# A decoder layer with attention and 16 experts: row numbers and gates copied out of the x buffers, a table in pieces, w2 loaded in seven parts

## What is computed

```python
x = x + attention_1(layernorm(x))                     # a linear attention
x = x + cross_attention(layernorm(x), ctx, ctx)       # 16 heads of 64, causal softmax
h = layernorm(x)
logits = h @ router_w + router_b                      # 16 experts
topw, topi = top_k(softmax(logits), 4); topw = topw / sum(topw)
for e in range(16):                                   # w1: 256x512, w2: 512x256
    out += (gelu(h @ w1[e] + b1[e]) @ w2[e] + b2[e]) * combine[:, e]
x = x + out
```

## Time and profile before

| | us |
|---|---|
| median of 3 runs (lowest, highest) | 1790.92 (1786.67, 1793.47) |
| the profiled execution | 1796.25 |
| its span in the trace | 1794.5 |
| busy in the span: PE, DVE, ACT, POOL | 1619.9, 1185.7, 1073.4, 504.7 |

### The profile page before, as it was taken

How to read it: one execution, slowest core, us unless ns; L and a number is a source line. 1 busy time by engine, 2 the same in 40 slices (tenths; PEclk the granted TensorE clock), 3 DMA queues, 4 the chain that set the end, 5 groups by cost and what they waited for, 6 DMA issues and landing times. The chain is left out here.

```text
span 1794.5 us, 35579 instructions
## 1 busy us (share of the span) xinstructions
PE 1619.9 (90%) x12470; PEld 1353.1 (75%) x12470; DVE 1185.7 (66%) x2675; ACT 1073.4 (60%) x2699; POOL 504.7 (28%) x430
## 2 busy tenths in 40 slices
PE   5899889999999999999999999657989989889995
PEld 4888767777776777777767777447989989888885
DVE  6988766677677776776677766557555555555552
ACT  4555466766666666766676666444556656555563
POOL 2444300001302103012021030315444444444544
PEclk9999999999999999999999999858999999999998
DMA  3121110000201101001011010726787776676773
GB/s 93 36 83 71 61 35 1 1 25 4 83 1 44 44 1 63 24 17 71 1 50 37 1 63 1 235 78 162 179 204 157 163 157 147 152 160 144 153 160 60
DMA packets 94926, 144.52 MB, mean 81 GB/s; under 512 B 12528, under 2 KB 55072, under 8 KB 94752
## 3 DMA queue, kind: packets, MB, share of 16 engines
q1 hardware_dynamic: 64128, 101.40, 18.8%
q0 software_dynamic: 28896, 38.62, 11.6%
q10 hardware_dynamic: 1728, 2.23, 0.4%
HBM read 90.76 MB, written 51.46 MB: 79 GB/s over the span
## 5 line engine op out<-in xcount | busy, mean ns | idle before, releaser
L1299 ACT ACTIVATE xa_prob<-xa_S,xa_nmax 128x512 f32<-128x512 f32 (+3 forms) x512 | 265.9, 534 | 135.0 <-DVE xa_nmax L1409 123.7
L1695 PE MATMUL ex_H<-ex_xT,ex_w 128*128 128x256 f32 x1896 | 254.4, 292 | 5.7 <-DVE ex_xT L1774 5.7
L1695 PEld LDWEIGHTS ex_H<-ex_xT,ex_w 128*128 128x128 f32 x1896 | 240.1, 198 | 6.5 <-issue 6.5
L1709 PE MATMUL ex_Y<-experts_w_hi,ex_hT 128*128 x1264 | 239.6, 283 | 0.0
L1780 DVE TENSOR_TENSOR ex_hT<-ex_h,ex_hT 128x512 fp32r<-128x512 f32 x158 | 109.4, 693 | 154.9 <-ACT ex_hT L1735 142.5
L1409 DVE TENSOR_REDUCE xa_nmax<-xa_S 128x2 f32<-128x1024 f32 (+3 forms) x256 | 197.7, 813 | 8.6 <-remote 5.0
L1709 PEld LDWEIGHTS ex_Y<-experts_w_hi,ex_hT 128*128 128x128 f32 x1264 | 200.4, 189 | 0.0
L1569 POOL DMA_INDIRECT expert_rows<-kept_xn,kept_rows x116 | 112.1, 967 | 292.4 <-DVE xa_prob L1421 252.2
L1313 ACT ACTIVATE xa_probT<-xa_work 128x512 f32<-128x512 f32 x256 | 139.9, 602 | 82.5 <-PE xa_work L1184 80.1
L1709 PE MATMUL ex_Y<-experts_w_lo,ex_hT 128*128 x632 | 178.6, 283 | 0.0
L1421 DVE TENSOR_SCALAR xa_prob<-xa_prob,xa_sums 128x512 f32<-128x512 f32 (+3 forms) x512 | 169.4, 384 | 6.8
(11 more groups left out here) (352 smaller groups left out, 3764.7 us busy)
## 6 DMA issues: line engine op xcount, KB each, us to landing
ahead_ctx<-in_w SPq DMA_DIRECT2D x27, 512.0 KB, 3.9
ahead_x<-in_w SPq DMA_DIRECT2D x26, 512.0 KB, 4.1
ahead_xn<-in_w SPq DMA_DIRECT2D x26, 512.0 KB
kept_x<-expert_rows SPq DMA_DIRECT2D x32, 273.0 KB, 3.1
kept_xn<-expert_rows SPq DMA_DIRECT2D x31, 273.0 KB
experts_w_lo<-in_w SPq DMA_DIRECT2D x4, 2048.0 KB, 9.5
ex_x<-expert_rows SPq DMA_DIRECT2D x16, 273.0 KB
expert_rows<-ahead_spare SPq DMA_DIRECT2D x32, 136.5 KB
```

The lines of the kernel that those rows point to most:

```text
L1299: m = act.activation(prob[n % 2][:, odd, PROB_AT[i]:PROB_AT[i] + width], SB[slot[at]][:, odd, col:col + width], ACT.Exp, bias=nmax[n % 2][ ...
L1695: m = pe.matmul(bank[:, (f % 2) * ROWS:(f % 2 + 1) * ROWS], ww[:, c, f * P:(f + 1) * P], xx[:, c, :], start=(i == 0), stop=(i == len(terms ...
L1709: m = pe.matmul(bank[:, a * D:(a + 1) * D], hh[:, f, a * P:(a + 1) * P], W2[:, bass.ds(own * WE + f * D, D)], start=(i == 0), stop=(i == l ...
```

## The change

It does the following.

1. Copies. In the step `transpose` of tile j, DVE first copies the row numbers and gates (17 columns of each of the two rows per partition) from the x buffer into one of five `tail`s, after waiting for x of tile j and for the add of tile j-5. ACT and GpSimd read gates and row numbers from there. The load of x into the buffer of tile j-5 waits for PE's transposes and for this copy, and no longer for the eviction of y and the add.
2. The late table. `work_out` is cut into `count_tiles`, `find_owners` and `find_rows`, done by DVE after steps 5, 7 and 9; PE's transposes follow in step 12, ahead of tile 12's hidden matmuls, DVE's copies at the end of step 12, and PE's transposes of tile 14 wait for them. Padding moves one step back.
3. The first table. It is worked out after the turns of pair 63, and turned and copied behind the last norm (`tables_turn`), with `first_loads` behind it.
4. w2. Seven loads of two or three experts, in the last batch's pairs 4 to 7, each after the projections and scores that use its place. The casts go in the order 3, 4, 5, 6, 7, 14, 15, 0, ...: four ahead of pair 63's weighing, eight behind it, four behind the last x transposes. 13 of 16 low halves are formed ahead of the barrier, three behind it, after step 0's low halves.
5. The barrier. SP waits for b1T, which it loads ahead of the barrier, and not for the store of x2; ACT waits for that store before its first eviction of y. The gelu table is loaded ahead of the barrier. Tiles and buffers change places in SBUF so that the store and the load of b1T run into nothing in use.

The diff, cut to its core:

```diff
+        self.used, self.warm = sb("used", [P, E]), sb("warm", [P, 1])
+        self.b1T = ahead.bits[:].rearrange("p a b -> p (a b)").bitcast(F32)[:, 0:E * FC]
...
-    def work_out(self, dve, w, done, part, ahead, kept, count):
+    def count_tiles(self, dve, w, done, part, kept, count):
...
+    def find_owners(self, dve, w, done, part, number, kept):
...
+    def find_rows(self, dve, w, done, part, number, kept, count):
...
-W2_LOADS, LOW_W2 = 4, 10
+LOAD_W2 = ((2, 5), (5, 8), (12, 14), (14, 16), (8, 10), (10, 12), (0, 2))
+OF_LOAD = {e_: i for i, (first, last) in enumerate(LOAD_W2) for e_ in range(first, last)}
+W2_ORDER, LOW_W2 = (3, 4, 5, 6, 7, 14, 15, 0, 1, 2, 8, 9, 10, 11, 12, 13), 13
...
-            plan += turns + finish + scatters
+            plan += [*turns, ("tables", None), *high_w2(0, 4), finish[0], *low_w2(0, 3), finish[1], *scatters]
...
-        elif p == 6:
-            second.append(("load_w2", None))
-        elif p == 7:
-            second.append(("tables", None))
+        else:
+            second += {4: [("load_w2", 0)], 5: [("load_w2", 1)], 6: [("load_w2", i) for i in (2, 3)],
+                       7: [("load_w2", i) for i in (4, 5, 6)]}.get(p, [])
...
-             *(("high_w2", e_) for e_ in range(E)), *low_w2(0, 3), ("output", (b, 1, 0)), *low_w2(3, 5), ("output", (b, 1, 1)),
-             ("first_loads", None), ("find3", b), ("norm3", b), ("transpose_x3", (b, 0)), ("transpose_x3", (b, 1)),
-             *low_w2(5, LOW_W2), ("route", b), ("choose", b), ("mark", b), ("weigh_gates", b), ("place", b), ("turn_gates", b),
+             *high_w2(4, 12), *low_w2(3, 6), ("output", (b, 1, 0)), *low_w2(6, 8), ("output", (b, 1, 1)), ("find3", b), ("norm3", b),
+             ("tables_turn", None), ("first_loads", None), ("transpose_x3", (b, 0)), ("transpose_x3", (b, 1)),
+             *high_w2(12, E), *low_w2(8, LOW_W2), ("route", b), ("choose", b), ("mark", b), ("weigh_gates", b), ("place", b), ("turn_gates", b),
...
-                    w.wait_ge(q_pe, B * PAIRS - 1)
...
+                    end, (first, last) = B * PAIRS - 1, LOAD_W2[at]
+                    w.wait_ge(k_pe, end - PAIRS)
+                    w.wait_ge(v_pe, v_tiles[-1])
+                    w.wait_ge(k_pe, end, at >= 2)
+                    w.wait_ge(s_pe, (end - 1, 1, 1), at >= 3)
+                    w.wait_ge(q_pe, end, at >= 4)
+                    w.wait_ge(s_pe, (end, (3, 2, 1)[at - 4], 1) if at >= 4 else None, at >= 4)
+                    sp.dma_start(f32(W2_lo[:, first * WE:last * WE]).rearrange("p (k n) -> p k n", n=D),
+                                 d['w2'][first:last].rearrange("e (k p) n -> p (e k) n", p=P)).then_inc(w2_in[at].of(at), 16)
                 elif step == "first_loads":
+                    w.wait_ge(pos_pe, B - 2)
+                    sp.dma_start(kept.b1T, d['b1T']).then_inc(b1_in.of(0), 16)
...
-            w.wait_ge(x2_out, B - 1)
+            w.wait_ge(b1_in, 0)
...
-                    w.wait_ge(pv_pe, (B * PAIRS - 1, 1))
-                    w.wait_ge(w2_in[at * W2_LOADS // E], at * W2_LOADS // E)
+                    w.wait_ge(s_pe, (B * PAIRS - 1, 1, 1))
+                    w.wait_ge(pv_pe, (B * PAIRS - 2, 1))
+                    w.wait_ge(pv_pe, (B * PAIRS - 1, 1), W2_ORDER.index(at) >= 4)
+                    w.wait_ge(w2_in[OF_LOAD[at]], OF_LOAD[at])
...
+                    if b == B - 1:
+                        act.activation(kept.warm[:], number[:], ACT.Gelu)
...
-                    tables.work_out(dve, w, t_dve, 0, ahead, kept, routing["count"])
+                    tables.count_tiles(dve, w, t_dve, 0, kept, count)
+                    tables.find_owners(dve, w, t_dve, 0, number, kept)
+                    tables.find_rows(dve, w, t_dve, 0, number, kept, count)
+                elif step == "tables_turn":
...
-        plan = [("load_w1", 2), ("load_x", 2), ("split_w1", 0), ("transpose", 0), ("split_w1", 1), ("load_w1", 3), ("low_w2", None)]
+        plan = [("load_x", 2), ("load_w1", 2), ("split_w1", 0), ("transpose", 0), ("split_w1", 1), ("load_w1", 3), ("load_x", 3)]
+        late = {5: ("count_tiles", None), 7: ("find_owners", None), 9: ("find_rows", None)}
         for j in range(MOE_TILES + 1):
-            plan += [("load_x", 3)] if j == 0 else []
-            plan += [(step, at) for step, at in (("load_w1", j + 4), ("load_x", j + 4), ("transpose", j + 1), ("hidden", j),
-                                                 ("split_w1", j + 2), ("results", j - 1)) if 0 <= at < MOE_TILES]
-            plan += [("tables", None)] if j == 4 else []
-            plan += [("pad", e_) for e_ in (2 * (j - 5), 2 * (j - 5) + 1) if 0 <= e_ < E]
+            step_of = {"load_w1": j + 4, "load_x": j + 4, "transpose": j + 1, "hidden": j, "split_w1": j + 2, "results": j - 1}
+            for step, at in step_of.items():
+                plan += [(step, at)] if 0 <= at < MOE_TILES else []
+                plan += [("turn_tables", None)] if step == "transpose" and j == TURN_AT else []
+                plan += [("low_w2", e_) for e_ in W2_ORDER[LOW_W2:]] if step == "hidden" and j == 0 else []
+            plan += [("give_tables", None)] if j == TURN_AT else []
+            plan += [late[j]] if j in late else []
+            plan += [("pad", e_) for e_ in (2 * (j - 6), 2 * (j - 6) + 1) if 0 <= e_ < E]
...
-            sp.dma_start(b1T, d['b1T']).then_inc(b1_in.of(0), 16)
...
-                    w.wait_ge(y_ev, j - NX, j >= NX)
-                    w.wait_ge(added[(j - NX) % NY], (j - NX, RT - 1), j >= NX)
+                    w.wait_ge(tail_set, j - NX, j >= NX)
...
-                if step == "tables":
-                    w.wait_ge(x_hi, 4)
-                    w.wait_ge(x_lo, 4)
+                if step == "turn_tables":
+                    w.wait_ge(x_hi, TURN_AT)
+                    w.wait_ge(x_lo, TURN_AT)
                     tables.transpose(pe, w, t_dve, XB[0], ident).then_inc(tables_pe.of(0), 1)
                 elif step == "transpose":
                     bank = XB[j % 2]
                     w.wait_ge(x_loaded[j % NX], j, j >= FIRST)
                     w.wait_ge(x_lo, j - 2, j >= 2)
-                    w.wait_ge(t_dve, ("landed", 2), j == 6)
+                    w.wait_ge(t_dve, ("landed", 2), j == TURN_AT + 2)
...
+                    w.wait_ge(x2_out, B - 1)
                     w.wait_ge(added[j % NY], (j - NY, RT - 1), j >= NY)
-                    w.wait_ge(x_loaded[j % NX], j, j >= FIRST)
+                    w.wait_ge(tail_set, j)
                     w.wait_ge(t_dve, ("landed", 2), j >= SURE_TILES)
                     own = act.value_load(owner_i[0:1, j:j + 1], min_val=0, max_val=E - 1)
                     for a in range(RT):
                         i = act.activation(y[j % NY][:, a, :], YB[j % 2][:, a * D:(a + 1) * D], ACT.Copy,
-                                           scale=x_in[j % NX][:, a, bass.ds(own + GATE, 1)])
+                                           scale=tail[j % NT][:, a, bass.ds(own + GATE - D, 1)])
...
-                    for e_ in range(LOW_W2, E):
...
-                elif step == "tables":
+                    mine = slice(j * WE, (j + 1) * WE)
+                    dve.tensor_tensor(W2_lo[:, mine], f32(W2_lo[:, mine]), f32(W2_hi[:, mine]), op=ALU.subtract
+                                      ).then_inc(low_w2.of(j), 1)
+                elif step == "count_tiles":
                     dve.tensor_tensor(pad_i[:], routing["count"][0:1, :], ahead.region[:], op=ALU.add).then_inc(pad_at.of(0), 1)
-                    tables.work_out(dve, w, t_dve, 1, ahead, kept, routing["count"])
+                    tables.count_tiles(dve, w, t_dve, 1, kept, routing["count"])
+                elif step == "find_owners":
+                    tables.find_owners(dve, w, t_dve, 1, ahead.number, kept)
+                elif step == "find_rows":
+                    tables.find_rows(dve, w, t_dve, 1, ahead.number, kept, routing["count"])
+                elif step == "give_tables":
                     w.wait_ge(tables_pe, 0)
                     tables.give_out(dve, t_dve, 1, XB[0], ahead, routing)
                 elif step == "split_w1":
                     w.wait_ge(w1_loaded[j % NW], j, j >= FIRST)
-                    w.wait_ge(b1_in, 0)
...
+                    w.wait_ge(x_loaded[j % NX], j, j >= FIRST)
+                    w.wait_ge(added[(j - NT) % NY], (j - NT, RT - 1), j >= NT)
+                    dve.tensor_copy(tail[j % NT], x_in[j % NX][:, :, D:PAY]).then_inc(tail_set.of(j), 1)
...
-                    w.wait_ge(x_loaded[j % NX], j, j >= FIRST)
+                    w.wait_ge(tail_set, j)
...
-                        pool.indirect_dma_start(out, bass.IndirectOffsetOnAxis(x_in[j % NX][:, a, ID:ID + 1].bitcast(I32), 0),
+                        pool.indirect_dma_start(out, bass.IndirectOffsetOnAxis(tail[j % NT][:, a, 0:1].bitcast(I32), 0),
```

(12 more changed lines are left out.)

64 lines of the change are left out of this document (27 added, 37 removed).

## The result

The changed kernel takes **1733.04 us** (median of 4 runs, 1730.92 to 1737.16), where the kernel before takes 1788.80 beside it: a ratio of 0.969, 95% interval 0.966 to 0.972. The forecast was 1728, from 1714 to 1753. In three later groups of runs on other chips the same pair gave 0.965 (0.960 to 0.970), 0.967 (0.964 to 0.970) and 0.972 (0.969 to 0.976). So the sign, the size and the range held, and each time the gain is between 50 and 60 us where 62.7 was forecast.

A forecast was written before the change was run, and what follows sets the result against it. In the expert stage the loop of x loads waiting for scatter-adds, not PE, was taken to set the pace (6.95 us a tile against 6.18). The terms summed to -62.7 from 1790.92, giving 1728 us, range 1714 to 1753.

The forecast's parts named there:

- The x loads, -54.6: Expert tiles: x loads wait for DVE's tail copy instead of an add, so all 45 PE waits, 54.6 us, go.
- What comes late next, +8 (5 to 14): Tiles 41 to 60: chained adds fall 18 us behind PE; part is borne, 8 us of stalls stay.
- the slack: Tail copy on DVE: 4 us spare before the add is awaited, about 4 more before PE needs DVE; 8 to 13 borne.
- The late table, -9.3 + 3 + 1.5: Tiles 6 and 7 gain 9.3 us; the turn at tile 12 costs 3, pieces sticking out of DVE's free time 1.5.
- the step of 9 us at tile 13: Expert tiles: sign of a right forecast, one step of about 9 us at tile 13.
- Pads, +3: Expert tiles that store pads: denser DMA keeps eight steps from quite running at PE's pace, +3 us (0 to 6).
- Handover, -12 (7 to 16): From attention to experts: later first table -8, turns and clock -5.5, w2 casts ahead of an eviction +1.5; 12 us gained.
- The 4.5 us for the five turns and 1 for the clock: Handover: 4.5 us back from ACT's five slow evictions if PE keeps its clock, 1 from the output projection.
- the handover gives nothing: Rival: slow turns have an unnamed cause, half clock may stay, casts may cost what the table did; 1740 us, chance 0.07.
- Barrier, 0: Barrier before the experts: SP's removed wait was hidden by GpSimd's drain, so nothing gained, at most 0.3 us.
- Opening, -2.3 (0 to 4): First expert tiles: b1T already there and fewer low halves give 5 us, later x for tile 4 takes 2.5 back.
- The rival of adds that become the bound: Rival, 16 chained expert-stage adds: each takes 1 us longer to land, 16 us more, 1744 us; chance 0.21.

The follow-up runs named there:

- second profile of before: The unchanged kernel before, run and profiled again on a quicker chip: 1787.17 us, ratio to itself 1.0006; handover 61.8 us.
- 4th of the changed kernel: The changed kernel unaltered, profiled a fourth time, as reference on a chip where the kernel before takes 1805.2 us: 1754.89 us, ratio 0.972.
- (d): Group of runs on one chip: the kernel before, nothing changed, once more for a second profile: 1787.17 us, ratio to itself 1.0006.
- (a): Group of runs on one slower chip: the changed kernel, unaltered, as reference 1746.34 us, the kernel before 1805.6 us.
- (b): Group of runs on one quicker chip: the changed kernel, unaltered, as reference 1732.55 us, the kernel before 1789.0 us.
- (c): Group of runs on one slower chip: the changed kernel, unaltered, as reference 1754.89 us, the kernel before 1805.2 us.

## Why the prediction was right, and where not

**The x loads, -54.6: the right cause.** All waits went. Putting the wait for the add back costs 36 (profiles) to 48 us (medians); by the sum it would be 43.6, the 54.6 less the 8 for late adds and the 3 for pads. The size of the one term is not shown: it is the idle time of the weight loads, and that of the matmuls behind them was 45.3.

**What comes late next, +8 (5 to 14): the right thing, forecast at less than half its size.** The main place, the engine and the order of events were as forecast: the adds of tiles 41 to 60 fall behind, DVE stops at the tail's copy, PE behind it. But it costs 17 to 23 us at tiles 54 to 67, and 3 to 7 at tile 12, which the sum did not have. Two steps of the sum failed. The first is the slack: 8 to 13 us were to be borne. PE first stops at tile 54 or 55, when the adds are some 9 us behind, so that much is right; but with the stop the chain itself becomes slower. From the first add of tile 40 to that of tile 60 it takes 140.0 us in the kernel with the copy two tiles later and 141.0 and 141.2 with four y buffers, close to the forecast 142; in the changed kernel it takes 145.3 to 150.7. The likely reason is in these rows of DVE and GpSimd:

```profile
1570.94 0.18 DVE L1804 COPY ahead_bits<-kept_xn 128x34 f32<-128x34 f32 x1 [5.70 <-DMA out<-ex_y,ahead_bits]
1571.04 0.68 DVE L1806 TENSOR_TENSOR ex_xT<-ex_X,ex_xT 128x512 fp32r<-128x512 f32 x1
...
1571.64 1.28 DVE L1812 TENSOR_TENSOR ex_hT<-ex_h,ex_hT 128x512 fp32r<-128x512 f32 x2
1571.73 2.10 POOL L1844 DMA_INDIRECT out<-ex_y,ahead_bits  x1 [5.13 <-POOLq L1840]
...
1572.84 0.90 DVE L1793 CAST ex_w<-ahead_ctx 128x1024 fp32r<-128x1024 f32 x1
1573.78 1.23 DVE L1795 TENSOR_TENSOR ex_w<-ahead_ctx,ex_w 128x1024 fp32r<-128x1024 f32 x1
1574.14 2.30 POOL L1844 DMA_INDIRECT out<-ex_y,ahead_bits  x1 [0.30 <-issue]
...
1574.92 0.16 DVE L1800 COPY ex_b<-ahead_bits 128x4 f32 x1
```

When the adds are that late, DVE and GpSimd wait for the same landing. Both start within 0.8 us of each other, DVE with everything that has piled up, and the two issues take 2.10 and 2.30 instead of 1.55. Over the adds of tiles 41 to 61 a mean issue is 1.86 to 1.90 us in the changed kernel, 1.68 in before, and 1.75 where the copy stands two tiles later; for the 40 issues of 20 tiles the last difference makes 4 to 6 us (an estimate), of the 5 to 11 by which the chain is longer. Such issues are no novelty: 2.30 stands at 1576.51 in before too. New is that DVE's wait makes them come one after the other. The Trainium skill, "SBUF — State Buffer", section "Who interferes with whom", has the rule by which copies on DVE hold up GpSimd's descriptors. The first issue agrees with it: a cast overlaps it and itself takes 0.90 instead of 0.69. The second does so less plainly, since beside it stand only the end of a subtraction and a copy of 0.16; which of DVE's instructions holds an issue up, no run separates. The prediction applied the rule to the new copy of the tail alone, and not to the burst that the new wait lets loose.

The second failure is the opening. The adds of tiles 1 to 7 are late as well: their first issues come 27 to 33 us after their tile's transposes, where 21 is undisturbed; in the code each of tiles 1 to 4 waits for the adds before it, up to two, whatever its expert. The longest wait of DVE at the copy up to tile 12 is 4.8 us. The sum looked for late adds only where the rows of before showed a chain, behind tile 40.

**The late table, -9.3 + 3 + 1.5: right in each part, wrong as a sum.** Tiles 6 and 7 gain 7.3 and 2.0 as read from the earlier trace rows, the turn costs 2.8 at tile 14. But the table in one piece gives the same time from tile 0 to 78: the pause had covered the stall that now comes at tile 12. (The prediction's list of signs puts the step of 9 us at tile 13; it is at tile 14, as in its sum.)

**Pads, +3: none.** At a DMA share of 0.91 (1240 to 1260 us) tiles took 6.18, and in the kernel with four y buffers all steps but that of tile 14 are at 6.1 to 6.2 there.

**Handover, -12 (7 to 16): about -7.** Its first term was right, 8 forecast and 7.2 measured by putting the table back; the four w2 casts ahead of pair 63's eviction cost 1.2 by the rows (6.97 us from pair 62's eviction to it in the first profile of the changed kernel, 5.81 in the second of before; no run takes them out), 1.5 forecast. The 4.5 us for the five turns and 1 for the clock do not come out of the change, and this is the step that failed here: they were read from the earlier trace rows, where each of ACT's evictions waits. Here are the same evictions in the second profile of before, and then three of the five in the 4th of the changed kernel ("remote" is a release that the profile cannot name):

```profile
1154.66 2.23 ACT L1313 ACTIVATE xa_probT<-xa_work 128x512 f32<-128x512 f32 x4
1156.79 0.59 ACT L1310 ACTIVATE xa_probT<-xa_work 128x512 f32<-128x512 f32 x1
```

```profile
1156.68 0.60 ACT L1329 ACTIVATE xa_probT<-xa_work 128x512 f32<-128x512 f32 x1 [0.90 <-PE xa_work L1200]
1159.56 0.60 ACT L1329 ACTIVATE xa_probT<-xa_work 128x512 f32<-128x512 f32 x1 [2.28 <-remote]
1163.12 0.60 ACT L1326 ACTIVATE xa_probT<-xa_work 128x512 f32<-128x512 f32 x1 [2.97 <-remote]
```

Before can have its turns back to back, and the changed kernel can have them slow. From pair 62's eviction to pair 63's it takes 5.8 us in one profile of before and 13.8 in the other, 7.0 in two of the changed kernel and 12.6 and 15.8 in the two others. Compared like with like, short with short (61.8 against 54.5 and 56.0), the handover gains 7.3 and 5.8; long with long (69.1 against 59.0 and 64.1) 10.1 and 5.0. The rival "the handover gives nothing" had named just this, a cause that no row names, at 0.07.

**Barrier, 0: right.** SP's drain, 2.9 us behind the start of GpSimd's in the earlier trace rows, is now 0.1 ahead of it, and GpSimd's still ends last, at 1186.8:

```profile
L1597 SPq DRAIN  x1: 7/7/7, 1182.6 to 1182.6; - x1
L1597 POOLq DRAIN  x1: 4109/4109/4109, 1182.7 to 1182.7; - x1
```

**Opening, -2.3 (0 to 4): not settled.** In the first pair of profiles tiles 0 to 5 gain 1.8 us (33.80 to 32.01); in the other profiles of the changed kernel they take 32.4, 32.7 and 34.5, in the second of before 33.5. The wait behind the low halves of the earlier trace rows was not removed but moved: PE waits 3.5 ahead of tile 0's results, and the run with the low halves first takes it away.

**The total.** By the profiles the change gains 30.6 us at tiles 7 to 78 (39.1 in the sum), 10.1 at tiles 0 to 7 (11.6) and 6 to 7 in the handover (12), 47 in all less about 1 at the end. The medians say 50 to 60. The 4 to 13 us between the two are not located: the executions with a profile are single ones, and tiles 54 to 67 alone differ by 6 us between them. Some of it is which executions were profiled: that of before in (d) is 4.5 us under the median of its runs, those of the changed kernel in (a), (b) and (c) are 1.5 to 3.6 above theirs. The forecast came within 5 us of 1733 although its stalls were 14 to 19 us too small and its gain in the handover 5 to 6 too large. That is in part luck: the median moved more than the profiles do. The ends of the range were also added up too wide on the bad side: the terms' bad ends make some -42, so 1749, where the sum says -38 and 1753.

The rival of adds that become the bound had 0.21 and 1744, by a landing that takes 1 us longer. What happened lies between it and the forecast, and its mechanism was, as far as the rows show, a longer issue, not a longer landing: GpSimd's waits at L1840 are 4.1 us each (48.7 in 12), and 4.1 in before (41.4 in 10, 1510 to 1650 us).

## What to carry to other kernels

When a wait is moved to another engine, count what stands behind it there, and ask who else waits for the same event: two engines that one landing releases start together, and here each was slower beside the other. A copy that frees a buffer belongs as late in its engine's queue as its readers allow, behind everything that the bottleneck needs; here that move, one more tail and one more y buffer were worth another 24 to 26 us, though one x buffer was given up for them. Before a wait without a named releaser is priced, look at a second execution.

## What was not expected of the hardware

Executions of the same program come with two lengths of attention, 876.4 to 877.7 us and 884.6 to 888.2, whichever kernel it is. The difference comes in seven steps of about 1.3 us, most of them in the last pair of a batch; at the three that were looked at, one reduction of DVE starts that much later. Here is the first of the three in the first profile of before, and the same instruction in the second:

```profile
463.80 1.02 DVE L1409 TENSOR_REDUCE xa_nmax<-xa_S 128x2 f32<-128x512 f32 x2 [1.22 <-remote]
```

```profile
462.55 1.01 DVE L1409 TENSOR_REDUCE xa_nmax<-xa_S 128x2 f32<-128x512 f32 x2
```

Together with it the evictions of the last turns are slow, and in (a) and (c) PE waits 2.9 to 7.4 us ahead of a weighing in the handover, for nothing that the profile names. In groups (a) and (c), where the kernel before takes 16 to 19 us longer, all seven profiles are of the long kind, in (b) and (d) all five of the short one; the first profile of before was long and that of the changed kernel short. The order of instructions on PE, ACT and DVE through the seven batches is the same in both kernels, so the change is not the cause. What is, stays open.
